# Six of eight batches of the last expert layer sorted by expert, two kept dense, with ten experts of the second dense batch among the sorted batches' preparation

## The reference, cut to what matters

```
logits = norm(x) @ Wg.T                     # 256 -> 16
scores = sigmoid(logits); s = scores + bias
the two best of four groups of four experts stay (by the sum of their two best s)
topk_idx = the 4 best experts in them; topk_w = their scores / (sum + 1e-20) * 2.5
out = sum over the 4 experts of topk_w * (relu(norm(x) @ W1[e].T) ** 2) @ W2[e].T     # 256 -> 128 -> 256
x = x + out + (relu(norm(x) @ Ws1.T) ** 2) @ Ws2.T                                    # the shared expert, 256 -> 256 -> 256
```

## Time and profile before

| | |
|---|---|
| median of 3 runs | 3158.94 us (3150.52 to 3166.24) |
| the profiled execution | 3162.49 us, its span 3160.6 us |
| PE busy, share of the span | 2702.3 us, 85% |
| DVE, ACT, POOL busy | 2132.8, 1586.8, 1181.4 us |
| granted PE clock, mean | 0.933 |
| DMA | 262.88 MB, mean 83 GB/s |

### The profile page before, as it was taken

The page is one execution under the profiler, slowest core; times in us unless marked ns, Lnnn a source line. Parts: engine busy times, 40 slices in busy tenths (PEclk is TensorE's granted clock), DMA queues, the critical chain, the costliest instruction groups (busy, mean ns, idle before and its releaser), DMA issues.

```text
span 3160.6 us, 39455 instructions
## 1 busy us (share of the span) xinstructions
PE 2702.3 (85%) x13080; PEld 1625.4 (51%) x13142; DVE 2132.8 (67%) x4071; ACT 1586.8 (50%) x2357; POOL 1181.4 (37%) x874
## 2 busy tenths in 40 slices
PE   7778878887765689999886999967989988999999
PEld 4445544454443255555544666644444445666666
DVE  1688889788886777877633222227887876777776
ACT  3678778778872245555541111127787781111111
POOL 0788888888882221111101000024455430100000
PEclk9899999899877799999998999988988999999999
DMA  3578878788784765555605000020000002000000
GB/s 114 114 169 148 180 170 161 155 179 168 150 189 96 195 177 102 81 86 87 96 14 188 24 24 22 19 56 7 8 14 7 8 1 61 7 14 7 7 7 14
DMA packets 122343, 262.88 MB, mean 83 GB/s; under 512 B 14785, under 2 KB 76993, under 8 KB 120481
## 3 DMA queue, kind: packets, MB, share of 16 engines
q0 software_dynamic: 28000, 134.89, 20.9%
q1 hardware_dynamic: 94144, 125.47, 17.3%
HBM read 135.40 MB, written 131.20 MB: 84 GB/s over the span
## 4 chain that ended last, share of the span: by engine, by line
PE 47%; DVE 7%; issue 7%; ACT 3%; POOL 2%; DMA 1%; POOLq 0%; DVEq 0%; ACTq 0%
PE PS L2384 7%; PE PS L1676 6%; PE PS L2402 6%; PE PS L1970 3%; PE PS L1698 3%; PE PS L2014 3%; PE PS L1339 2%; PE PS L2032 2%; PE PS L1297 1%; PE PS L1267 1%; PE PS L1321 1%; PE PS L1318 1%; DVE PS L1527 1%; POOL Z L2229 1%; ACT Z L2100 1%
## 5 line engine op out<-in xcount | busy, mean ns | idle before, releaser
L856 POOL TENSOR_TENSOR Z<-Z 128x1024 f32<-128x1024 f32 x256 | 645.2, 2722 | 123.7 <-DVE Z L757 78.6
L764 DVE TENSOR_TENSOR_SCAN Z<-PS,Z 128x1024 f32<-128x1024 f32 x256 | 576.4, 2274 | 20.7 <-ACT PS L684 10.4
L535 PE MATMUL PS<-Z 128*128 128x128 f32 x2048 | 301.4, 293 | 119.9 <-DVE Z L764 48.2
L535 PEld LDWEIGHTS PS<-Z 128*128 128x128 f32 x2048 | 248.3, 150 | 253.0 <-issue 84.1
L684 ACT ACTIVATE PS<-Z 128x511 f32<-128x511 f32 x512 | 332.8, 688 | 65.0 <-DVE Z L764 63.5
L1527 DVE CUSTOM_DVE_ANT_0 PS<-PS,Z 128x512 f32<-128x512 f32 (+3 forms) x512 | 242.2, 511 | 122.5 <-PE PS L1297 117.4
L1435 ACT ACTIVATE Z<-PS 128x512 f32<-128x512 f32 x320 | 188.7, 596 | 254.8 <-PE PS L1321 251.8
L2435 ACT ACTIVATE Z<-PS 128x512 f32<-128x512 f32 x144 | 85.9, 597 | 411.9 <-PE PS L2384 411.9
L696 ACT ACTIVATE Z<-PS,Z 128x512 f32<-128x512 f32 x378 | 245.9, 684 | 77.2 <-PE PS L535 69.1
L2384 PE MATMUL PS<-Z 128*128 128x512 f32 x576 | 273.5, 600 | 7.9 <-DVE Z L2517 7.1
L2100 ACT ACTIVATE Z<-Z 128x2048 f32<-128x2048 f32 x128 | 249.9, 1994 | 34.1 <-PE PS L2014 21.8
(11 more groups left out here) (293 smaller groups left out, 4896.5 us busy)
## 6 DMA issues: line engine op xcount, KB each, us to landing
sums<-Z POOLq DMA_DIRECT2D x112, 768.0 KB, 8.2
Z<-rows_b SPq DMA_DIRECT2D x128, 256.0 KB, 4.7
Z<-scr SPq DMA_DIRECT2D x256, 128.0 KB, 5.5
rows_n<-in_L_ffn_expert_wv POOLq DMA_DIRECT2D x32, 528.0 KB, 7.4
scr<-Z SPq DMA_DIRECT2D x32, 384.0 KB
Z<-Z POOLq DMA_DIRECT2D x14, 768.0 KB, 7.3
Z<-in_L_ffn_expert_wv SPq DMA_DIRECT2D x4, 2048.0 KB, 14.7
Z<-sums SPq DMA_DIRECT2D x7, 768.0 KB, 6.4
```

The lines of the kernel that those rows point to most:

```text
L535: ins = e.transpose(self.turned[i % 2][:, c * 128:(c + 1) * 128], self.h(k, c // 2)[:, c % 2, i * 128:(i + 1) * 128], ident)
L764: e.tensor_tensor_scan(h, a, h, 0.0, ALU.mult, ALU.add).then_inc(s["scan"], 1)
L856: e.tensor_tensor(self.h(k, f), self.du[b % 2][:, 2 * f:2 * f + 2, :], b3(self.Bs[k % 2], 1, [128, 2, 512]), ALU.mult).then_inc(s["hin"], 1)
```

## The change

The last layer now has two kinds of batches. Batches 0 to 5 are routed: only the four chosen experts of a token are computed for it. Batches 6 and 7 stay dense. The stage has three lists, `first`, `pairs` and `last`, walked one after the other.

`first` has a preparation of eight steps for each batch, a new batch every six steps (`h`), in the order `SEQ` 0, 1, 2, 6, 3, 7, 4, 5. Of a routed batch, ACT writes the normalized tokens four times, once for each chosen expert (`norm`); DVE chooses by `max` and `max_index` (`choose`), PE counts places in each expert's region (`places`), DVE makes the row numbers (`spots`), POOL issues 16 indirect scatters of 128 rows of 258 numbers (token, weight, destination row) to `rows_e` (`spread`). The shared expert of each batch is done here too. The dense work of batch 6 (16 experts) and of ten experts of batch 7, together 78 steps, is put in from h = 27 to 49, 3.25 steps for each h, the rest at the end. After batch 5's `spots`, `table` computes which expert and which rows each slot of 128 rows has; SP writes 16 blocks of 128 zero rows behind the regions' ends, with addresses from registers.

`pairs` works 112 slots in 56 pairs: SP gathers the slots into 24 buffers (register address), PE transposes (`heads`), DVE copies the transposed tokens out of PSUM and copies the expert's W1 (256 columns, register address) beside them, PE multiplies (`ups`), ACT takes the relu, DVE multiplies by PSUM, PE multiplies by W2 (register address, `downs`), ACT scales, POOL scatters 128 rows of 256 numbers to `rows_z` by two indirect DMAs for each pair.

`last` has the other six experts of batch 7, and `yadd`: SP loads 2 MB of results for a routed batch back, in three buffers, and DVE adds the four parts of each token to x. The square of a dense `hidden` is now taken by ACT (Square) in place of DVE. The lines of the diff that matter:

```diff
+        self.rows_e = nc.dram_tensor("rows_e", [16 * StageE.CAP + 16 * 128, StageE.ROW], F32, kind="Internal").ap()
+        self.rows_z = nc.dram_tensor("rows_z", [4 * 512 * StageE.R + 32 * 128, 256], F32, kind="Internal").ap()
...
+    NE, R, CAP, NG = 16, 6, 6 * 512 + 128, 24
+    NS = 16 * R + 16
+    NQ = NS // 2
+    ROW = 258
+    SEQ = (0, 1, 2, 6, 3, 7, 4, 5)
+    EARLY = 10
...
+    PREP = ((0, ("stats",)), (1, ("rstd",), ("minus",)), (2, ("norm",)), (3, ("flip",), ("flipped",)), (4, ("logits",), ("sig",)),
+            (5, ("choose",)))
+    ROUTED = ((5, ("hidden", 0)), (6, ("places",), ("hidden", 1)), (7, ("spots",), ("spread",), ("down", 0, 0), ("down", 0, 1)))
+    DENSE = ((5, ("hidden", 0)), (6, ("hidden", 1)), (7, ("down", 0, 0), ("down", 0, 1)))
...
+        self.src = [src[:, part * q:part * (q + 1)].rearrange("p (i j c) -> p i j c", j=4, c=self.ROW) for q in range(3)]
+        self.yb = [src[:, 4096 * q:4096 * (q + 1)].rearrange("p (i n) -> p i n", n=1024) for q in range(3)]
...
+        self.pairs = [("heads", 0), ("heads", 1)]
+        for t in range(self.NQ + 3):
+            for what, q in (("heads", t + 2), ("ups", t), ("downs", t - 3)):
+                if 0 <= q < self.NQ:
+                    self.pairs.append((what, q))
...
+    def dense(self, b, xs):
+
+        out, last = [], xs[-1]
+        for x in xs:
+            ahead = range(x, min(x + 3, last + 1)) if x == xs[0] else range(x + 2, min(x + 3, last + 1))
+            out += [("hidden", b, j + 2) for j in ahead]
+            out += [("down", b, x + 1, 0), ("down", b, x + 1, 1)]
+        return out
...
+        first, work = [], self.dense(6, range(16)) + self.dense(7, range(self.EARLY))
+        units = len(work)
+        start, last = 6 * self.SEQ.index(6) + 8, 6 * len(self.SEQ) + 2
+        for h in range(last):
+            for k, b in enumerate(self.SEQ):
+                plan = self.PREP + (self.ROUTED if b < self.R else self.DENSE)
+                for at, *steps in plan:
+                    if at == h - 6 * k:
+                        first += [(s[0], b) + s[1:] for s in steps]
+                        first += [("table",)] * (("spots",) in steps and b == self.R - 1)
+            upto = max(0, h - start) * units // (last - start)
+            while units - len(work) < upto:
+                first.append(work.pop(0))
+        first += work
+        final = []
+        for n, step in enumerate(self.dense(7, range(self.EARLY, 16))):
+            final.append(step)
+            if n % 3 == 2 and n // 3 < self.R:
+                final.append(("yadd", n // 3))
+        return first, final
...
+        for q in range(4):
+            at = 16 * self.CAP + 512 * q
+            e.dma_start(m.rows_e[at:at + 512].rearrange("(a r n) c -> a r (n c)", a=4, r=32),
+                        d["pads"][16 + 4 * q:20 + 4 * q].rearrange("a (r n) c -> a r (n c)", r=32)).then_inc(s["d_fill"], 16)
+        out = m.out.rearrange("b (i p) c -> b p i c", p=128)
+        e.wait_ge(s["ends"], 1)
+        for x in range(16):
+            at = e.value_load(self.ends[0:1, x:x + 1], min_val=0, max_val=16 * self.CAP - 128)
+            e.dma_start(m.rows_e[bass.ds(at, 128)], d["pads"][x]).then_inc(s["d_fill"], 16)
+        e.wait_ge(s["slot"], 1)
+        e.wait_ge(s["d_fill"], 16 * 20)
+        for q in range(3):
+            e.wait_ge(self.d_spread[q], 256 * (self.R // 3))
+        for c in range(self.NS):
+            if c >= self.NG:
+                e.wait_ge(*self.scattered(c - self.NG))
+            at = e.value_load(self.slot[0:1, 128 + c:129 + c], min_val=0, max_val=16 * self.CAP + 15 * 128)
+            e.dma_start(self.g[:, c % self.NG, :], m.rows_e[bass.ds(at, 128)]).then_inc(self.d_g[c % self.NG], 16)
+            if c == 3:
+                e.wait_ge(s["acc"], self.u1)
+                e.dma_start(out[6], m.X[:, 24:28, :]).then_inc(m.d_out, 16)
+        for c in range(self.NS - 8, self.NS):
+            e.wait_ge(*self.scattered(c))
+        for b in range(self.R):
+            if b >= 3:
+                e.wait_ge(s["yadd"], b - 2)
+            e.dma_start(self.yb[b % 3], m.rows_z[2048 * b:2048 * (b + 1)].rearrange(
+                "(i p j) c -> p i (j c)", p=128, j=4)).then_inc(self.d_back[b % 3], 16)
+            if b >= 3:
+                e.dma_start(out[b - 3], m.X[:, 4 * b - 12:4 * b - 8, :]).then_inc(m.d_out, 16)
+        for b in range(self.R - 3, self.R):
+            e.wait_ge(s["yadd"], b + 1)
+            e.dma_start(out[b], m.X[:, 4 * b:4 * b + 4, :]).then_inc(m.d_out, 16)
+        e.wait_ge(s["acc"], len(self.dnx))
+        e.dma_start(out[7], m.X[:, 28:32, :]).then_inc(m.d_out, 16)
...
+        def heads(q):
+            if q < 2:
+                e.wait_ge(*ring.done(self.n_ring - 1))
+                e.wait_ge(*ring.done(self.n_ring - 2))
+            else:
+                e.wait_ge(s["hs"], q - 1)
+            for h in range(2):
+                e.wait_ge(*self.loaded(2 * q + h))
+                for k in range(2):
+                    ins = e.transpose(self.hb[q % 2][:, 256 * h + 128 * k:256 * h + 128 * (k + 1)],
+                                      self.g[:, (2 * q + h) % self.NG, 128 * k:128 * (k + 1)], ident)
+            ins.then_inc(s["ht"], 1)
+
+        def ups(q):
+            e.wait_ge(s["hs"], q + 1)
+            if q < 3:
+                e.wait_ge(s["relu"], self.n1)
+                e.wait_ge(s["acc"], self.u1)
+            else:
+                e.wait_ge(s["pm"], q - 2)
+            for h in range(2):
+                c = 2 * q + h
+                expert[c] = e.value_load(self.slot[0:1, c:c + 1], min_val=0, max_val=15 * 256)
+                for k in range(2):
+                    ins = e.matmul(self.ub[q % 3][:, 128 * h:128 * (h + 1)], self.wq[q % 4][:, 256 * h + 128 * k:256 * h + 128 * (k + 1)],
+                                   self.hs[q % 4][:, 256 * h + 128 * k:256 * h + 128 * (k + 1)], start=k == 0, stop=k == 1)
+            ins.then_inc(s["pu"], 1)
+
+        def downs(q):
+            e.wait_ge(s["pm"], q + 1)
+            if q >= 3:
+                e.wait_ge(s["py"], q - 2)
+            for h in range(2):
+                ins = e.matmul(self.db[q % 3][:, 256 * h:256 * (h + 1)], self.hm[q % 4][:, 128 * h:128 * (h + 1)],
+                               self.w2f[:, bass.ds(expert.pop(2 * q + h), 256)], start=True, stop=True)
+            ins.then_inc(s["pd"], 1)
+
+        self.walk(self.pairs, {"heads": heads, "ups": ups, "downs": downs})
+        self.walk(self.last, {"hidden": hidden, "down": down})
...
+        def norm(b):
+            s6, mv, r = self.sb
+            e.wait_ge(s["nb"], self.k(b) + 1)
+            if 3 <= b < self.R:
+                e.wait_ge(self.d_spread[b % 3], 256 * (b // 3))
+            if b == 7:
+                e.wait_ge(s["prod"], self.uses["flip", 6, 1] + 1)
+            for i in range(4):
+                x = m.X[:, 4 * b + i, :]
+                if b < self.R:
+                    o, x = self.src[b % 3][:, i, :, 0:256], b3(x, 1, [128, 4, 256])
+                else:
+                    o = self.nt[:, i, :]
+                ins = e.activation(o, x, ACT.Identity, bias=self.nb[:, i:i + 1], scale=r[:, i:i + 1])
+            ins.then_inc(s["nt"], 1)
...
+            if n >= 6:
+                e.wait_ge(s["dn"], self.read[n - 6])
+            e.wait_ge(s["relu"], n + 1)
+            e.activation(self.hd[n % 6], self.rr[n % 3], ACT.Square).then_inc(s["hid"], 1)
+
+        def ups(q):
+            e.wait_ge(s["pu"], q + 1)
+            e.activation(self.rp[q % 4], self.ub[q % 3], ACT.Relu).then_inc(s["pr"], 1)
+
+        def downs(q):
+            e.wait_ge(s["pd"], q + 1)
+            if q >= 4:
+                for c in (2 * q - 8, 2 * q - 7):
+                    e.wait_ge(*self.scattered(c))
+            for h in range(2):
+                ins = e.activation(self.yo[q % 4][:, 256 * h:256 * (h + 1)], self.db[q % 3][:, 256 * h:256 * (h + 1)], ACT.Copy,
+                                   scale=self.g[:, (2 * q + h) % self.NG, 256:257])
+            ins.then_inc(s["py"], 1)
...
+        def choose(b):
+            e.wait_ge(*ring.done(self.uses["logits", b, 0]))
+            step(e.tensor_scalar(scf, scf, 1.0, None, ALU.add))
...
+            for i in range(4):
+                ins = e.max(self.v8[:, i, :], ms[:, i, :])
+            step(ins)
+            for i in range(4):
+                ins = e.max_index(self.ix8[:, i, :], self.v8[:, i, :], ms[:, i, :])
+            step(ins)
+            step(e.tensor_copy(self.ixf, self.ix8[:, :, 0:4]))
+            step(e.tensor_tensor(oh, b3(self.ixf.rearrange(FLAT), 2, [128, 16, 16]), b3(self.iota, 1, [128, 16, 16]), ALU.is_equal))
+            oh4, tmp4 = (x.rearrange("p (i j) e -> p i j e", j=4) for x in (oh, tmp))
+            step(e.tensor_tensor(tmp4, oh4, sc.unsqueeze(2).to_broadcast([128, 4, 4, 16]), ALU.mult))
+            if b < R:
```

(57 more changed lines are left out.)

458 lines of the change are left out of this document (258 added, 200 removed).

## The result

The changed kernel took 3188.07 us (median of four runs, 3181.8 to 3190.08) beside 3160.1 us for the kernel before: a ratio of 1.0081, 95% interval 1.0062 to 1.0100. I had forecast no difference at 3156 us. The time is inside my range and beyond half a per cent: slower, and not what I forecast. It is also not the whole answer: in two of the five jobs run afterwards the same code, or variants of it, was late in the same way (1.0056 and 1.0091 for the unedited kernel), and in three it was 2% faster than the kernel before (unedited 0.9798, 0.9775 to 0.9821, in one of these). What parts the two kinds of job is the subject of most of this text.

The account below looks back on a forecast made before the run. PE's columns bound the last stage before; after the change no engine bounds it all. Preparation to 247 us, pairs from 275 to 487, then the end gave 545 against 548.4: no difference, 3156 us, range 3125 to 3190.

Parts of the forecast that it names:

- The preparation, 247 us: List `first`, from the stage's start to batch 5's last `spots`: 247 us, with POOL's scatters of 20 us a batch beside it.
- the ring: Dependent steps of one routed batch in the preparation, from `minus` to the next batch's `minus`: 29 us a batch.
- The gap, 28 us: From the last `spots` at 247 us to the first pair at 275: table, 16 blocks at 1.3 us, landing, first gathers.
- The pairs, 212 us: List `pairs`: 56 pairs at 3.6 us, plus 3 to start and 7 to drain, PE with its register loads the limit.
- My 3.6: Time of one pair in us, limited by PE and its register loads with some clock loss; bounds 3.0 and 4.9.
- Rival A: In the pairs, register loads hide in the queues and the clock stays up: 3.0 us a pair, 3115 us; chance 0.27.
- The end, 58 us: List `last`, after the pairs: scatters and landing 6, first rows back 7, DVE's additions 40, stores and end 5 us.
- The sum: The whole last stage: 545 us against 548.4 before, 3 us less, forecast as no difference.
- D: Rival in the preparation: `choose` with dense neighbours costs 7 us more for each of four batches, 28 us, 3184; chance 0.07.
- B: Rival in the pairs: POOL sets the pace at 4.1 us a pair, 3184 us; chance 0.08.
- C: Rival in the pairs: PE's clock falls; half clock 4.9 us a pair, 3229; half the time so, 4.25 and 3192; chance 0.13.

Follow-up runs that it names:

- e15: The changed kernel, unedited, run again in the fifth job, where signals were on time: 3098.7 us, 0.9798 of the kernel before.
- e10: The changed kernel with only one of every 16 `spread` scatters, constant blocks gathered, in a late job: 3140.7 us, 0.9924 of the kernel before.
- e7: The changed kernel with POOL scattering only one of the two slots of each pair, in a late job: 3127.8 us, 0.9897 of the kernel before.
- e3: The changed kernel with the 16 blocks of pads shared between SP's and ACT's queues, in an on-time job: 3093.4 us, 0.9781 of the kernel before.
- e8: The same kernel as e3 (pads on two queues), run again in a late job: 3184.3 us, 1.0055 of the kernel before.
- jobs 1 and 2: First two sets of follow-up runs, on the same chip: job 1 on time (3093.4 to 3107.8 us), job 2 late (unedited changed kernel 3179.7 us).
- 3 and 4: Third and fourth sets of follow-up runs, on the same chip: job 3 late (unedited changed kernel 3194.0 us), job 4 on time (3097.5 to 3106.9 us).

## Why the prediction failed, by its own steps

**The preparation, 247 us.** This is the step that failed: I wrote that POOL's scatters, 20 us a batch, "lie beside it", and costed them at nothing. In the late jobs each burst costs the ring 7 us. Periods between `minus`: 30.1, 34.4, 34.4, 26.1, 34.6, 38.3, 38.0 us late; 30.1, 27.7, 27.6, 19.2, 34.5, 31.8, 37.4 on time (e15); 29, 29, 29, 22, 31, 34, 36 forecast. The end of the preparation is at 279 us late and at 245 on time, where my 247 was right as a sum; single periods were up to 3.5 us off, and in both directions. The late signal at the logits is 4.7 us of the 6.7; signals at `down` that came some 2 us late in the same bursts are the likely rest. The trail stood in the trace of before, in the earlier layer's scatters, of which I read only their price.

**The gap, 28 us.** 28.3 on time: 20.23 us for 16 blocks is 1.26 each, and I had taken 1.3. 39.8 late, for one block is then 1.98 by the mean. e10, late but with one scatter, has 27.8: the same cause.

**The pairs, 212 us.** Too dear in both kinds: 190 late, 148 on time. Windows of e15 (columns as above): the preparation, the pairs, the end.

```profile
2610.00:2865.00 255.00, 197.59 (x744) 130.56 (x741) 132.56 (x521) 97.79 (x156) 79.72 (x87) 0.87 0.21 70
2900.00:3030.00 130.00, 124.77 (x833) 108.91 (x831) 86.67 (x210) 61.94 (x152) 92.31 (x95) 1.00 0.68 203
3035.00:3100.00 65.00, 32.27 (x96) 20.56 (x95) 38.77 (x49) 11.74 (x23) 12.71 (x14) 0.76 0.68 262
```

On time two engines are full at once. From pair 10 to pair 50 POOL begins one every 2.56 us, back to back (two of 0.96 + 0.30, no longer than the earlier trace rows has them), and PE one every 2.52 at a granted clock of 1.00; POOL's scatters fall behind ACT's results from 0.3 to 3.5 us over the 56 pairs. Which of the two would set the pace without the other was not measured in a job on time; e7, late and with half of the pairs' scatters, has 139.2 us for 56, or 2.49 each. My 3.6 counted the register loads as idle time of PE, 2 x 0.45 us. The load takes 0.31 us by the median on PE and DVE in either kind, but other matmuls cover it: PE is busy 124.77 of 130. Rival A (3.0 us a pair, 3115 us) named just this and was nearest to the jobs on time. In the late jobs a pair takes 3.4 us (189.8 for 56), and e7 shows that the scatters cost it; PE waits more, up to 1.38 us at a time in the window of 2950 to 3100 us, and the granted clock there is 0.94.

**The end, 58 us.** DVE's chain took 39 us (40 forecast), the stores 5. But it began 20 to 21 us after PE's last `downs` instead of 13: POOL was some eight scatters behind PE, 10 us that I had costed as two (2.5).

**The sum.** Late: 545 + 32 + 12 - 22 + 6 = 573, measured 572.4. On time: 545 - 2 + 0 - 64 + 7 = 486, measured 486.4 (e15). That 3188 us lies inside my range of 3125 to 3190 is luck: 50 us were missing in three terms, and a pairs term that was 22 too dear took a part of them back.

**The rivals.** D named 28 us in the preparation and 3184 us, near to what came, by another mechanism: it wanted the dense neighbours, and the batches without any are just as late. B is false as put: scatters took 960 ns beside the W1 copies of 339. C is false: 0.94 and 1.00. The Trainium skill's case of the clock that falls in each round's wait (TensorE: Matmul & The Clock Gate, HAM oscillation) did not arise in the pairs on time: from 2900 to 3030 us of e15 the longest idle stretch of PE is 0.78 us, and the granted clock is 1.00.

## What stays open

What makes a job late or on time is not known: not the code (e3, e8), not the chip (jobs 1 and 2, 3 and 4), and the kernel before runs at the same time in both. Nor is it shown why TensorE's signals and SP's steps are held while those of DVE and ACT reach the next engine as fast as on time (`minus` to `norm` 0.04 us, `norm` to the transposes 0.05 where nothing else is waited for, in both). Where the program's or the rows' memory lies in a job would fit, but no run shows it. The split burst and the plain stores were not tried in a late job.

One rival is left untested: the recording itself. Every run on record has the span and the granted clock of its core, so each was recorded, and the late traces are those that lack 14 to 21% of their landing records, most of them of the scatters and of the gathers beside them. Either something that the scatters fill up holds the signals and loses the records, or the writing of the records takes part in holding the signals up. No run here tells these apart, so it isn't shown that an execution that nobody records would be late.

## To carry to other kernels

Work that lies beside the critical path on another engine is not free until the trace shows the two together: look in the kernel before for the same kind of instruction, and whether what runs beside it is signalled on time ("remote" in ACT's or DVE's idle time). Measure a change that adds many indirect scatters in several jobs; one job would here have said 0.8% slower or 2.0% faster. For a loop over engines, take the fullest engine's own work as the pace, and count the backlog of a slow last engine at its end.

## Of the hardware, unexpected

- In three jobs of six, TensorE's signals at the logits came 3.8 to 9.4 us late beside bursts of 16 indirect scatters from SBUF to DRAM, and SP's register steps took up to 0.7 us; by the count, which takes missing records for late ones, 168 of 280 signals beside such scatters were over 0.3 us late in the profile after, and 2 of 297 in e15. The same traces lack 14 to 21% of the landing records.
- A register load from SBUF takes 0.31 us by the median on PE and DVE, 0.27 on SP's blocks; on PE other matmuls covered it (busy 124.77 of 130 us).
- Two float32 additions with all operands in SBUF, one on DVE and one on POOL, don't share time: the one that starts second waits until the first is over (DVE 2.86 and 2.98 us in place of 1.22, POOL 2.86 in place of 2.00).
